# Scores of a head's second query tile by one matmul over both halves of k, and the masked low part in the tile's own probability buffer

## The reference

```
logits = jnp.einsum('bhqd,bhkd->bhqk', q, k)
causal = jnp.tril(jnp.ones((s, s), dtype=bool))[None, None]
logits = jnp.where(causal, logits, MASK_VAL)
logits = logits / jnp.sqrt(jnp.float32(HEAD_DIM))
attn = jax.nn.softmax(logits, axis=-1)
out = jnp.einsum('bhqk,bhkd->bhqd', attn, v)
```

## Time and profile before

| | |
|---|---|
| median of three executions | 1062.06 us |
| the profiled execution | 1062.15 us, its span 1060.3 us |
| PE busy | 1042.1 us, 98% |
| PE weight loads | 865.9 us, 82% |
| DVE busy | 758.5 us, 72% |
| ACT busy | 639.0 us, 60% |
| POOL busy | 416.1 us, 39% |
| matmuls and weight loads | 5495 each |
| scores of tiles i = 1 (128x256) | 128 matmuls, 28.0 us busy |

### The profile page before, as it was taken

The page is one execution under the profiler, slowest core; times in us unless marked ns, Lnnn a source line. Parts: engine busy times, 40 slices in busy tenths (PEclk is TensorE's granted clock), DMA queues, the critical chain, the costliest instruction groups (busy, mean ns, idle before and its releaser), DMA issues.

```text
span 1060.3 us, 20102 instructions
## 1 busy us (share of the span) xinstructions
PE 1042.1 (98%) x5495; PEld 865.9 (82%) x5495; DVE 758.5 (72%) x2138; ACT 639.0 (60%) x1454; POOL 416.1 (39%) x422
## 2 busy tenths in 40 slices
PE   7999999999999999999999999999999999999996
PEld 6888888888888888888888888888887888888884
DVE  8677777776666767666666767666667777777777
ACT  6667777776665766666665656666685333334333
POOL 4153443434252544434352534434466232233221
PEclk9999999999999999999999999999999999999999
DMA  7122324232311346021011202021232323332311
GB/s 279 40 85 71 129 69 134 69 130 59 101 56 30 109 169 228 16 71 50 30 49 35 69 10 69 10 74 48 92 132 59 120 80 100 119 111 87 99 60 61
DMA packets 58663, 90.36 MB, mean 85 GB/s; under 512 B 3568, under 2 KB 36336, under 8 KB 58608
## 3 DMA queue, kind: packets, MB, share of 16 engines
q1 hardware_dynamic: 58464, 89.44, 25.7%
q10 hardware_dynamic: 144, 0.26, 0.1%
HBM read 64.52 MB, written 25.17 MB: 85 GB/s over the span
## 4 chain that ended last, share of the span: by engine, by line
PE 94%; DVE 1%; ACT 1%; issue 1%; POOL 1%; DVEq 0%; ACTq 0%; POOLq 0%
PE bank L1477 50%; PE bank L1408 24%; PE bank L1508 6%; PE bank L1527 3%; PE bank L1526 3%; PE bank L1642 2%; PE bank L1619 1%; PE bank L1450 1%; PE bank L1643 1%; PE bank L1529 1%; PE bank L1493 1%; PE bank L1438 1%; POOL big_lo L660 1%; PE bank L1420 0%; DVE stats L1187 0%
## 5 line engine op out<-in xcount | busy, mean ns | idle before, releaser
L1477 PE MATMUL bank<-big_hi,w_hi 128*128 128x512 f32 (+1 forms) x776 | 325.8, 420 | 0.3 <-DVE big_lo L1037 0.3
L597 POOL TENSOR_SCALAR prob<-prob,rinv 128x128 f32<-128x128 f32 (+3 forms) x256 | 136.6, 533 | 445.7 <-DVE rinv L1072 445.0
L1477 PE MATMUL bank<-big_hi,w_lo 128*128 128x512 f32 (+1 forms) x776 | 304.5, 392 | 0.0
L1477 PE MATMUL bank<-big_lo,w_hi 128*128 128x512 f32 (+1 forms) x776 | 302.8, 390 | 0.0
L742 ACT ACTIVATE prob<-prob,nmax 128x128 f32<-128x128 f32 (+3 forms) x256 | 143.9, 562 | 212.1 <-DVE nmax L1062 210.3
L1477 PEld LDWEIGHTS bank<-big_hi,w_lo 128*128 128x128 f32 x776 | 145.6, 188 | 32.8
L1477 PEld LDWEIGHTS bank<-big_hi,w_hi 128*128 128x128 f32 x776 | 146.5, 189 | 19.7 <-issue 0.4
L1477 PEld LDWEIGHTS bank<-big_lo,w_hi 128*128 128x128 f32 x776 | 147.1, 190 | 11.6
L1062 DVE CUSTOM_DVE_ANT_0 prob<-bank,mask 128x256 f32<-128x256 f32 (+2 forms) x192 | 106.1, 553 | 35.4 <-PE bank L1408 28.0
L1080 DVE TENSOR_TENSOR pT_lo<-bank,pT_hi 128x128 fp32r<-128x128 f32 (+3 forms) x256 | 124.3, 486 | 2.6 <-ACT pT_hi L753 2.4
L1508 PE MATMUL bank<-ident,prob 128*128 128x128 f32 x640 | 111.7, 272 | 1.3 <-DVE pT_lo L1080 0.8
(11 more groups left out here) (148 smaller groups left out, 1894.5 us busy)
## 6 DMA issues: line engine op xcount, KB each, us to landing
w_raw<-in_wqkv SPq DMA_DIRECT2D x48, 512.0 KB, 4.5
attention_out<-o_sum SPq DMA_DIRECT2D x64, 128.0 KB, 2.3
w_raw<-attention_out SPq DMA_DIRECT2D x16, 512.0 KB, 4.7
land<-in_x SPq DMA_DIRECT2D x16, 512.0 KB, 3.5
out<-res SPq DMA_DIRECT2D x14, 512.0 KB, 2.6
xin<-in_x SPq DMA_DIRECT2D x12, 512.0 KB, 5.7
xT_hold_hi<-xin SPq DMA_DIRECT2D x8, 512.0 KB, 3.6
xT_hold_lo<-xn SPq DMA_DIRECT2D x8, 512.0 KB, 5.4
```

The lines of the kernel that those rows point to most:

```text
L597: pool.tensor_scalar(p, p, rinv[:, q % 4:q % 4 + 1], 1.0, ALU.mult, ALU.mult).then_inc(prob_done, 1)
L1477: done = pe.matmul(grp_ps[(b + k) % 2][:, cols], w, xt[:, cols], start=at == 0, stop=at == GROUP_MM - 1)
```

## The change

Tile i = 1 of every head now takes the path of tile i = 0. There are 64 such tiles (32 units, two heads). Its two matmuls of 256 columns become one of 512 columns over both halves of k, which fills a score bank. DVE adds the mask to the low block (128x256) in an instruction of its own. The sum no longer goes to `low_masked`, which is dropped, but to columns 256 and up of the tile's own row of `prob`, for tile 0 as well.

```
-        low_masked = sb(sB, "low_masked", [P, P])
...
                     added = mask[:, SEQ - n:SEQ]
-                    if q % QT == 0:
-                        added = low_masked[:, :]
-                        dve.tensor_tensor(added, sc_ps[0][:, P:2 * P], mask[:, SEQ - P:SEQ], ALU.add).then_inc(low_added, 1)
-                        dve.wait_ge(low_added, 2 * a + q // QT + 1)
+                    if q % QT < 2:
+                        added = prob[:, q % 4, 2 * P:2 * P + n]
+                        dve.tensor_tensor(added, sc_ps[q % 2][:, n:2 * n], mask[:, SEQ - n:SEQ], ALU.add).then_inc(low_added, 1)
+                        dve.wait_ge(low_added, 4 * a + 2 * (q // QT) + q % QT + 1)
                         dve.sem_inc(gate_dve, 1)
...
-                    if i == 0:
-                        pe.matmul(sc_ps[0][:, 0:2 * P].rearrange("p (a n) -> p a n", a=2), q_hl[:, ab, h, qc],
+                    if i < 2:
+                        pe.matmul(sc_ps[q % 2][:, 0:2 * P * (i + 1)].rearrange("p (a n) -> p a n", a=2), q_hl[:, ab, h, qc],
                                   k_all[:, :, ab, h, kc], start=True, stop=True).then_inc(s_done, 1)
```

## The result

The changed kernel takes 1071.43 us (median of six, 1070.9 to 1072.01) against 1062.05 us (six, 1061.91 to 1062.54): ratio 1.0088, 95% interval 1.0075 to 1.0101. It is 9.4 us slower. Forecast were 1069.5 us, slower, with 7.5 us on top of before. The profiled execution took 1070.9 us, its span 1069.1 us.

A forecast was written before the change was run, and what follows sets the result against it. PE's queue was taken to set the time (busy 98%), DVE costing only where PE waits for it. 0 + 6.0 + 0.6 + 0.9 = 7.5 us on 1062.06 gave 1069.5 us, range 1061.8 to 1073.5 us.

The forecast's parts named there:

- PE saves nothing: 0, bounds ±0.6 us: Score matmuls on PE: 512 columns cost the same as one matmul or two, so saving 0, ±0.6 us.
- One addition is 0.62 us: DVE, each tile i = 1: 0.42 us for the addition plus 0.20 us waiting for its own write.
- The crossing path has no slack: Unit 5 to 6, DVE's negate through ACT to PE's transposes: 0.62 us at the start becomes 0.62 us on PE.
- 6.0 us in units 1 to 9: Loss from 18 additions in units 1 to 9: 3.1, 2.0 and 0.9 us; bounds 1.5 to 11.2 us.
- the crossings: Odd to even unit, out of units 1, 3, 5, 7, 9: five times 0.62 us, 3.1 us.
- the waits at the earlier trace: PE's transposes in even ahead units 2, 4, 6, 8: 0.13 us of cover, 4 x 0.49 = 2.0 us lost.
- what I had put at 0.1 us each: The other 9 of 18 additions in units 1 to 9, meeting gaps or held instructions: 0.9 us together.
- 0.6 us in the closing slots: Closing slots, where PE already sat idle for pT_lo: no cover, +0.6 us, bounds 0 and 1.2 us.
- 0.9 us in ordinary units: 44 additions with 1.97 us of cover, lost only if POOL's w_lo holds DVE: 0.9 us, bounds 0 and 3.
- rival 3: Ordinary units: k_all or q_hl slips under POOL's w_lo, 0.3 us in each of 22, 6.6 us more, 1076 us; chance 0.06.
- Rival 1: DVE's idle 28% hides all the lateness before PE: 1062.1 us, up to 1064; chance 0.17.
- rival 2: Score matmul pairs: the second weight load was exposed, dropping it saves 10.1 us, giving 1059.5 us; chance 0.05.

The follow-up runs named there:

- the second head's run: Changed kernel, but with the change only for the second head's tile i = 1 (step 6, 32 additions): 1065.78 us, ratio 1.0034 to the kernel before.
- the run of its own: Changed kernel, but with the change only in units 0 to 9 (18 of 64 tiles): 1067.07 us, ratio 1.0046 to the kernel before.
- the first head's run: Changed kernel, but with the change only for the first head's tile i = 1 (step 2, 32 additions): 1065.55 us, ratio 1.0031 to the kernel before.
- the second run: Kernel before, two matmuls kept, plus DVE's extra 128x256 addition and its wait for tiles i = 1, sum unused: 1071.65 us, ratio 1.0090.
- the first: Changed kernel without DVE's added instruction and wait for tiles i = 1, wide matmul kept: 1061.88 us against 1062.12 us for the kernel before, ratio 0.9997.

## Why the prediction was right

Right was the mechanism, and with it the sign and the range; the sum was 1.9 us short (7.5 for 9.4 us).

- *PE saves nothing: 0, bounds ±0.6 us.* Shown: -0.24 us with an interval that holds 0. But the reason "cost goes with the columns alone" holds only down to 256 columns. A pair of 128 costs more. Only rows at 256 and 512 had been read, and nothing in them said that 128 would differ; that the change dealt with 256 was luck as far as this reason goes.
- *One addition is 0.62 us.* Measured 0.61 us.
- *The crossing path has no slack.* Shown link by link, 0.62 us for 0.62 us, and by the second head's run with 0.6 us at each crossing into units 2, 4, 6 and 8. The last one, into unit 10, let 0.33 us through in the changed kernel.
- *6.0 us in units 1 to 9.* Measured 4.95 us, by the starts as by the run of its own (the 5.35 us above hold 0.4 us at step 3 of unit 10, which the sum counted with the ordinary units). The parts were rougher than the sum: the crossings made 2.7 us for 3.1, the waits at the earlier trace rows about 0.5 for 2.0, and what I had put at 0.1 us each (step 3 and the first unit) about 1.7 for 0.9. That two misses of opposite sign nearly met is luck. They are partly one miss: in units 4 and 6 the same addition meets the wait at step 3 and then that of the earlier trace rows (the first head's run has both, the second head's neither), and what PE loses at the first (0.22 us in unit 4) is cover at the second. By that estimate 0.48 - 0.22 = 0.26 us are left in unit 4; measured are 0.25 us.
- *0.6 us in the closing slots, bound 1.2.* Measured 1.7 us, over the bound. The step of the prediction that failed is "the cover is nothing: +0.6 us": PE's stall at unit 32 grew by 1.1 us, not 0.6 us, since the additions of both heads reach it (0.6 and 0.5 us, worked out above from the runs with one head); that much the bound of 1.2 us allowed for. Another 0.6 us came at three other waits (0.24, 0.20 and 0.12 us), which the prediction did not look at. Ahead of them stands the long wait of unit 31; that it brings on a part of them is a reading of the order in time and not shown.
- *0.9 us in ordinary units.* Measured 2.6 us with unit 10's step 3, within its bounds (0 to 3) but nearly three times the term. The mechanism was named, the hold of k_all by POOL's w_lo, but the cover was taken from one wait and called that of the stretch. The earlier trace rows is the wait at step 1; the one at step 3 of an even unit had 1.13 us. With that row, 2 x 0.61 - 0.99 = 0.23 us at each of ten even units would have stood in the sum. The prediction had named "ordinary units grow" as a sign of being wrong, in favour of rival 3; the even ones did grow, by 0.35 us (24.30 for 23.95 us).

Rival 1 (all hidden) fell by the second run, rival 2 by the first. Rival 3, that the hold multiplies, was true in kind and smaller in size: 2.6 us in ordinary units for its 6.6 us on top. That it is the hold which joins the two additions rests on the timeline (k_all 0.64 us later against PE) and on the runs with one head; a run without the hold was not made.

## What to carry to other kernels

An instruction added on an engine that is idle a quarter of the time is not free when another engine's queue waits at that very point: follow the first consumer (here ACT's exponent) through everything queued behind it, to the wait of the engine that sets the time. Take the cover from every kind of wait in a period, not from one, and ask whether two delays of one period draw on the same cover. Before merging matmuls, read from starts what a pair and its merged form cost at that very width: here 2 x 256 into 512 gave nothing, 2 x 128 into 256 gives 0.11 us each.

## What the runs showed of the hardware

- A pair of matmuls of 128 columns with a weight load each costs 0.11 us more than one matmul of 256 columns; a pair of 256 costs the same as one of 512, 0.23 us. So somewhere between 128 and 256 columns lies the width from which the second matmul of a pair, with its weight load of 128x128, costs nothing but its columns in this kernel. The time is lost from the second of the pair on (0.17 us from the pair's start to the next matmul and 0.28 us to the one behind, for 0.11 and 0.23), not between the two of the pair, whose starts lie 0.06 us apart.
- DVE's wait for its own write before reading it back was 0.20 us in the mean at both sizes (12.5 and 12.2 us for 64 each in the changed kernel), and taking it out for tiles i = 1 was worth 6.0 us here (1071.43 to 1065.47 us). A few waits are longer: one in the changed kernel and two in the first head's run took 0.56 to 0.58 us.
